# Retention rebuilt in groups of four, its weights loaded ahead, and the residual added by TensorE through a product with the identity

## The reference

```python
x = x + _L0_attn_ref(_layernorm(x), ...)
x = x + _L0_xattn_ref(_layernorm(x), ctx_2048, ctx_2048, Wh, wg_w, wo_w, gn_gamma, gn_beta)

def _L0_xattn_ref(x, k, v, Wh, wg_w, wo_w, gn_gamma, gn_beta):   # two heads of 128
    Q, K, V = xh @ Wh, kh @ Wh, vh @ Wh                # per head
    scores = einsum('bshe,bthe->bhst', Q, K) / sqrt(128)
    masked = scores * Dn[None]                         # decay mask
    A = maximum(abs(masked.sum(axis=0)), 1.0)          # summed over all batches
    O = einsum('hst,bthe->bshe', A, V).reshape(b, s, dim)
    Y = (O - mu) / sqrt(var + GN_EPS) * gn_gamma + gn_beta
    W = relu(x @ wg_w)
    return W * Y @ wo_w
```

## Time and profile before

| | us |
|---|---|
| median of 3 runs | 1221.38 |
| lowest and highest | 1221.18 and 1222.14 |
| the profiled execution | 1221.15 |
| its span in the trace | 1219.4 |
| from the end of attention's last product to the start of the spline stage | 124.2 |

### The profile page before, as it was taken

One profiled execution on the slowest core, in us unless ns is written; L12 is line 12 of the kernel. 1 busy time (PEld: TensorE's weight loads), 2 busy tenths in 40 slices (PEclk: granted clock), 3 DMA queues, 4 the chain that ended last, 5 costly groups with the idle time before them and its releaser, 6 DMA issues. The chain is left out here.

```text
span 1219.4 us, 19890 instructions
## 1 busy us (share of the span) xinstructions
PE 1049.1 (86%) x6765; PEld 853.8 (70%) x6765; DVE 811.5 (67%) x1513; ACT 721.8 (59%) x2021; POOL 340.2 (28%) x274
## 2 busy tenths in 40 slices
PE   3799999999999999999386778189999689698997
PEld 2678788888788888888285566176777489574555
DVE  3888777777587767667355867957777634355775
ACT  3577776777567776766133255157777434456883
POOL 1344332332233332333000630124444310101442
PEclk9999999999899999999799577669999989899999
DMA  5111100000000000000440000000000000004442
GB/s 173 53 52 54 35 1 1 2 1 2 1 1 1 1 1 1 1 1 1 118 107 1 0 1 1 0 1 2 1 2 1 2 1 1 14 1 122 108 109 69
DMA packets 31161, 31.78 MB, mean 26 GB/s; under 512 B 8288, under 2 KB 23392, under 8 KB 30816
## 3 DMA queue, kind: packets, MB, share of 16 engines
q1 hardware_dynamic: 31072, 30.60, 9.1%
HBM read 28.36 MB, written 2.23 MB: 25 GB/s over the span
## 5 line engine op out<-in xcount | busy, mean ns | idle before, releaser
L310 POOL TENSOR_TENSOR roped_q<-roped_q,sin_q 128x512 f32<-128x512 f32 x64 | 82.0, 1282 | 323.9 <-DVE sin_q L442 323.9
L35 PE MATMUL banks<-xT_lo,WH 128*128 128x512 f32 x256 | 107.8, 421 | 8.8 <-issue 6.2
L1411 ACT ACTIVATE win_P<-banks,win_neg_max 128x128 f32<-128x128 f32 x256 | 91.2, 381 | 33.1 <-DVE win_neg_max L1477 32.8
L310 POOL TENSOR_TENSOR roped_k<-roped_k,sin_k 128x512 f32<-128x512 f32 x64 | 95.7, 1496 | 53.0 <-DVE sin_k L442 53.0
L349 ACT ACTIVATE P<-banks,neg_max 128x128 f32<-128x128 f32 x256 | 90.5, 370 | 29.7 <-DVE neg_max L465 29.7
L36 PE MATMUL banks<-xT_hi,WL 128*128 128x512 f32 x256 | 102.5, 401 | 0.0
L37 PE MATMUL banks<-xT_hi,WH 128*128 128x512 f32 x256 | 102.4, 400 | 0.0
L376 ACT ACTIVATE oT_hi<-banks,bv_col 128x512 fp32r<-128x512 f32 x64 | 44.1, 689 | 87.6 <-PE banks L586 87.6
L1370 POOL TENSOR_TENSOR win_P<-win_P,win_inv 128x512 f32<-128x512 f32 x64 | 66.7, 1042 | 104.4 <-DVE win_inv L1482 104.1
L358 ACT ACTIVATE sin_k<-banks 64x512 f32<-64x512 f32 x128 | 76.0, 594 | 10.3 <-PE banks L37 8.7
L358 ACT ACTIVATE sin_q<-banks 64x512 f32<-64x512 f32 x128 | 76.0, 593 | 8.0 <-PE banks L37 5.8
(11 more groups left out here) (352 smaller groups left out, 3145.1 us busy)
## 6 DMA issues: line engine op xcount, KB each, us to landing
moe_gate_of<-moe_gate_rows SPq DMA_DIRECT2D x32, 256.0 KB, 4.0
X<-in_x SPq DMA_DIRECT2D x4, 512.0 KB, 6.7
stage<-in_wqT SPq DMA_DIRECT2D x4, 512.0 KB, 3.8
stage<-in_wkT SPq DMA_DIRECT2D x4, 512.0 KB, 3.8
stage<-in_wvT SPq DMA_DIRECT2D x4, 512.0 KB, 6.1
stage<-in_woT SPq DMA_DIRECT2D x4, 512.0 KB, 3.7
ctx<-in_ctxT SPq DMA_DIRECT2D x1, 2048.0 KB, 10.9
out<-X SPq DMA_DIRECT2D x8, 256.0 KB, 2.8
```

Source lines behind the costliest of these rows:

```text
L35: nc.tensor.matmul(out, lh, rl, start=first, stop=False)
L310: nc.gpsimd.tensor_tensor(roped[w][:, p, :], roped[w][:, p, :], sin_part[w][:], ALU.add).then_inc(roped_sum[w], 1)
L1411: ins = nc.scalar.activation(P[:, h % 2, s, i, :], SC[2 * (h % 2) + s][:, i * 128:(i + 1) * 128], ACT.Exp, bias=neg_max[:, h % 2, at:at + ...
```

## The change

Attention: the last group's `add_out` and `add_const` leave the attention block. At step 12 of the last group DVE computes mean and variance of the first 12 batches, and POOL their rstd behind its last step. The tile `stage`, the bias and one semaphore now outlive the block, and once the last attention weight is split SP loads the retention's five weight arrays into `stage`. The semaphores of attention are freed ahead of the retention.

Retention is one block, all of it written out without loops. The first pass goes by groups of four batches: the product with G is 512 columns wide and made of three split products; the transposed x is rounded and split right from PSUM; PE reads the context where it was loaded, and it comes in four transfers, one a group; V and the gate go by pairs of batches; the gate is stored multiplied by gamma (`gain`) and by beta (`shift`). The last group's attention sum, bias and statistics lie in DVE's stream inside the first group. The second pass goes by pairs: two DVE operations a batch give gate * (gamma * y + beta), POOL has no elementwise work left, and the residual is a first fp32 product `ident x X` into the bank in which the output projection is summed; ACT copies the sum to X.

```diff
@@ attention, SP, after the last weights
+                sp.wait_ge(weights_split, len(ITEMS))
+                held = stage[:].rearrange("p s k n -> p (s k n)")
+                for i, src in enumerate((chunks("L0_xattn_wg_w"), chunks("L0_xattn_wo_w"))):
+                    sp.dma_start(held[:, 512 * i:512 * (i + 1)].rearrange(...), src).then_inc(ret_loaded, 16)
+                for i, src in enumerate((a["WhT"], a["L0_xattn_Wh"]..., a["decayT"])):
+                    sp.dma_start(held[:, 1024 + 256 * i:1280 + 256 * i]..., src).then_inc(ret_loaded, 16)
@@ attention, DVE
+                    if r == 12 and isinstance(g, int) and g == NG - 1:
+                        dve.wait_ge(restated, NEXT)
+                        finish_stats(nc, dve, ln0, B + 22, stats[:, 0:NEXT, :], ...)
                 run(dve, step)
-                add_out(NG - 1)
-                add_const(NG - 1)
@@ retention, SP
-                    sp.dma_start(dst, src).then_inc(consts, 16)
-                sp.dma_start(ctx_all[:], ...).then_inc(ctx_loaded, 16)
+                for g in range(NG):
+                    sp.dma_start(ctx[:, :, g * GW:(g + 1) * GW], ...).then_inc(ctx_loaded[g], 16)
+                    if g == 0:
+                        for i, name in enumerate(("L0_xattn_gn_gamma", "L0_xattn_gn_beta")):
+                            sp.dma_start(gn[:, i, :], ...).then_inc(gn_loaded, 16)
                 for dst, src in ahead:
                     sp.dma_start(dst, src).then_inc(ahead_loaded, 16)
@@ retention, ACT
+                for g in range(NG):
+                    take_T(g)
+                    if g + 1 < NG:
+                        round_xT(g + 1)
+                        take_V(2 * g + 2)
+                        take_V(2 * g + 3)
+                for p in range(PAIRS):
+                    take_O(p)
+                for p in range(PAIRS + 1):
+                    if p < PAIRS:
+                        round_wyT(p)
+                    if p > 0:
+                        take_out(p - 1)        # PSUM sum -> X
@@ retention, DVE
+                normalise(0)
+                TT_(flat(G_lo[:]), VB[:, 0:256], flat(G_hi[:]).bitcast(F32), ALU.subtract)
+                add_heads()                    # last group's attention sum
+                split_xT(0)
+                split_w(0)
+                dve.wait_ge(gn_loaded, 32)
+                for g in range(NG):
+                    if g + 1 < NG:
+                        normalise(g + 1)
+                    take_gate(2 * g)           # two 512-wide operations
+                    if g + 1 < NG:
+                        split_xT(g + 1)
+                    if g == 0:
+                        add_out_bias()         # and the statistics of batches 12 to 15
+                    if g == NG - 1:
+                        dve.wait_ge(scored, NG)
+                        ...                    # A
+                    take_gate(2 * g + 1)
+                    if g == 0:
+                        dve.wait_ge(stat, GROUP)
+                        n = finish_stats(...)
+                        split_w(1)
+                group_stats(FIRST2); finish_stats(...)      # batches 0 to 3, POOL's power behind it
+                group_stats(REST2); finish_stats(...)       # batches 4 to 15
+                scale(0)
+                for p in range(PAIRS + 1):
+                    if p + 1 < PAIRS:
+                        scale(p + 1)
+                    if p < PAIRS:
+                        split_wyT(p)
+                    if p > 0:
+                        restat(p - 1)
@@ retention, PE
+                transpose_x(0)
+                pe.wait_ge(G_split, 1)
+                project_V(0)
+                project_V(1)
+                for g in range(NG):
+                    project_T(g)
+                    if g + 1 < NG:
+                        transpose_x(g + 1)
+                    project_gate(2 * g)
+                    if g + 1 < NG:
+                        project_V(2 * g + 2)
+                    score(g)
+                    project_gate(2 * g + 1)
+                    if g + 1 < NG:
+                        project_V(2 * g + 3)
+                for p in range(PAIRS):
+                    mix(p)
+                for p in range(PAIRS + 1):
+                    if p < PAIRS:
+                        transpose_wy(p)
+                    if p > 0:
+                        project_out(p - 1)
+                def project_out(p):
+                    wait(pe, added, p - 1)
+                    nc.tensor.matmul(WOB[p % 2], ident[:], flat(pair(X, p)), start=True, stop=False)
+                    pe.wait_ge(wyT_lo_ready, p + 1)
+                    ...                        # twelve split products, 256 columns each
```

More of the change, by code:

```diff
@@ new lines, in normalise, with add_heads @@
+                def normalise(g):
+                    wait(dve, x_transposed, g)
+                    if g * GROUP >= EARLY:
+                        dve.wait_ge(rstd_ready, 1)
+                    for i in range(GROUP):
+                        b = GROUP * g + i
+                        TS(xn[:, i, :], X[:, b, :], mean[:, b:b + 1], rstd[:, b:b + 1], ALU.subtract, ALU.mult).then_inc(xn_ready, 1)
+                def add_heads():
+                    for i in range(2):
+                        some = slice(EARLY + 2 * i, EARLY + 2 * i + 2)
+                        TT_(X[:, some, :], by_batch(OUT0[i]), X[:, some, :], ALU.add).then_inc(heads_added, 1)
@@ new lines, in add_out_bias @@
+                def add_out_bias():
+                    for i in range(2):
+                        some = slice(EARLY + 2 * i, EARLY + 2 * i + 2)
+                        dve.wait_ge(heads_added, i + 1)
+                        TT_(X[:, some, :], X[:, some, :], two(out_bias[:]), ALU.add).then_inc(heads_added, 1)
+                    dve.wait_ge(heads_added, 4)
+                    for b in range(EARLY, B):
+                        nc.vector.bn_stats(stats[:, b, :], X[:, b, :]).then_inc(stat, 1)
@@ new lines, in group_stats, with scale @@
+                def group_stats(some):
+                    for b in range(some.start, some.stop):
+                        dve.wait_ge(O_ready, b // 2 + 1)
+                        nc.vector.bn_stats(stats[:, b, :], O[:, b, :]).then_inc(stat2, 1)
+                def scale(p):
+                    dve.wait_ge(rstd2_ready, 1 if 2 * p + 1 < GROUP else 2)
+                    wait(dve, wy_transposed, p)
+                    for b in (2 * p, 2 * p + 1):
+                        STT(O[:, b, :], O[:, b, :], mean[:, b:b + 1], gain[:, b, :], ALU.subtract, ALU.mult).then_inc(scaled, 1)
+                    for b in (2 * p, 2 * p + 1):
+                        dve.wait_ge(scaled, b + 1)
+                        STT(xn[:, b % 2, :], O[:, b, :], rstd[:, b:b + 1], shift[:, b, :], ALU.mult, ALU.add).then_inc(wy_ready, 1)
@@ new lines, in project_gate @@
+                def project_gate(p):
+                    if p == 0:
+                        pe.wait_ge(w_split, 1)
+                        pe.wait_ge(heads_added, 2)
+                    wait(pe, gate_ready, 2 * (p - 1))
+                    for b in (2 * p, 2 * p + 1):
+                        g, toks = b // GROUP, slice(b % GROUP * S, (b % GROUP + 1) * S)
+                        for k in range(KD):
+                            ins = matmul3(nc, GATE[p % 2][:, b % 2 * D:(b % 2 + 1) * D], (xT_hi[:, g % 2, k, toks], xT_lo[:, g % 2, k, toks]),
+                                          (w_hi[:, 0, k, :], w_lo[:, 0, k, :]), first=(k == 0), last=(k == KD - 1))
+                    ins.then_inc(gate_made, 1)
@@ new lines, in mix, with transpose_wy @@
+                def mix(p):
+                    wait(pe, O_ready, p - 3)
+                    for h in range(H_):
+                        ins = nc.tensor.matmul(by_batch(MIX[p % 4])[:, :, h * 128:(h + 1) * 128], AT[:, h, :], V[:, 2 * p:2 * p + 2, h, :], start=True, stop=True)
+                    ins.then_inc(mixed, 1)
+                def transpose_wy(p):
+                    pe.wait_ge(wy_ready, 2 * p + 2)
+                    wait(pe, wyT_lo_ready, p - 1)
+                    for k in range(KD):
+                        for j in range(2):
+                            at = (2 * k + j) * 128
+                            ins = nc.tensor.transpose(WYB[p % 2][:, at:at + 128], xn[:, j, k * 128:(k + 1) * 128], ident[:])
+                    ins.then_inc(wy_transposed, 1)
```

426 lines of the change are left out of this document (191 added, 235 removed).

## The result

The changed kernel takes **1179.1 us** (median of four runs, 1177.49 to 1182.2) against 1221.55 before (1221.18 to 1222.14): a ratio of 0.9655, with a 95% interval of 0.9634 to 0.9676. The forecast was 1184.0, with 1177 to 1196 as its range, so it is 4.9 too high. The profiled execution took 1178.37, its span is 1176.3.

A forecast was written before the change was run, and what follows sets the result against it. Bounds by part: DVE, late loads, PE with batch hand-over, a chain, DVE. Terms 0.3 + 9.4 + 37.8 + 11.7 + 27.6 = 86.8 against 124.2, 37.4 saved: 1184.0 us, range 1177 to 1196.

The forecast's parts named there:

- a PEclk of 0.50 in the output pass: Sign of being wrong: TensorE at its lower clock in the output pass, which would point to rival A.
- rival C: Clock never falls at the seam; V, G and first output pair at the upper clock: 4 less, 1180; chance 0.14.
- The seam: End of attention: 4.24 us become a 0.3 barrier, as the last group's sum, bias and statistics move away.
- To the first product with G: Second part, 9.4 us against 15.2: context load 5.2, then V for pairs 0 and 1 at the lower clock 4.2.
- rival B: The loads are late: context takes as long as the old seven loads, V starts at 599.5, 1188; chance 0.13.
- First pass: Four groups on PE 32.1, lower clock at the first G product 1.5, waits 4.2: 37.8 us against 46.6.
- The 1.5 for a low clock at the start: First pass: the first product with G runs at the lower clock and adds 1.5 us.
- the place where the seam's work went: First group: DVE has 10.0 us in one queue before group 2's transposes, so PE waits 3.5.
- Turning point: Between the passes: mix 7.1, then ACT, statistics, mean and variance, scale and hand-overs: 11.7 us against 18.0.
- Output pass: Second pass: pairs 3.0 apart, seven distances 21.0, plus the end: 27.6 us against 40.2.
- rival A: Output pass stays at the lower clock: a pair takes 5.2 against 3.0, 18 more, 1202; chance 0.12.
- Behind the spline stage: From the spline stage's start on, the change touches nothing; any change of time there would be a sign of being wrong.

The follow-up runs named there:

- seam_back: Against the changed kernel, the last group's head sum, output bias and statistics go back to attention's end, ahead of the new block; 1185.15 us.
- after: The changed kernel itself, in its first profile; median 1179.1 us.
- after_again: The changed kernel run and profiled once more, nothing altered, as reference for its set; 1179.6 us.
- late_weights: Against the changed kernel, the five early weight loads go back to the start of the retention block, ahead of the context; 1184.87 us.
- keep_busy: Changed kernel plus seven unread identity products on TensorE: five behind the mix, two between the first two output transposes; 1180.05 us.
- residual_dve: Against the changed kernel, DVE adds the residual in place of the identity product and ScalarE's copy; 1181.98 us.
- best: Changed kernel with group 2 normalised before the bias, seven unread products filling PE's pauses, and DVE's residual for the last two pairs; 1175.24 us.

## Why the prediction was right, point by point

Right in its sum and range, by parts of which two missed in opposite directions; that retention came out at 86.6 for 86.8 is luck to that extent. By its own list, two signs of being wrong turned up beside the right ones: a PEclk of 0.50 in the output pass, for two pairs, and a change of time behind the spline stage's start. The measured 1179.1 is nearer to rival C's 1180 than to 1184.0, but only C's terms for V and G came true. Its third, the first output pair at the upper clock, didn't, and the sum held no low clock for that pair: by the sum's own terms C is worth 3.2, not 4.

1. **The seam: right.** SP's first load comes 0.42 behind attention's last product. seam_back shows what the move was worth: 3.6 to 4.0 us in the sum. Of the 4.2, 0.85 is paid back as PE's wait in the first group, and the clock at V and behind that wait makes up the rest.
2. **To the first product with G: 7.07 for 9.4.** The terms that failed are the context's landing (4.3 for 5.2) and the clock of V. The prediction's rival C had the clock of V and G so, but for a reason that doesn't hold: the clock did fall at the seam, only ahead of it. In after it is at 0.50 from 587.5 to 590.9, in attention's last products, and V ran at 1.00. In after_again, the same kernel, it fell later, behind a pause of only 1.33:

```profile
590.00:595.70 5.70, 3.01 (x22) 2.33 (x23) 4.90 (x11) 2.71 (x5) 0.00 (x0) 1.00 0.74 227
595.70:599.10 3.40, 3.40 (x13) 3.01 (x14) 1.11 (x4) 0.93 (x2) 0.00 (x0) 0.50 1.02 326
```

There the second half of V takes 2.01 for 1.16, and the first product with G is slow as the prediction had it. Where PE paused for 4.29, in seam_back, all of V ran at 0.50. late_weights confirms the loads as the term that carried this part, at 4.3 to 4.7; rival B would have needed a late context, and there was none.
3. **First pass: 37.37 for 37.8, by other terms.** The group is 8.71 apart, the next 13.20, then 9.31, and 6.15 for the last; forecast 8.7, 12.2, 9.4, 6.0. The wait is at its place and from its queue, 2.72 for 3.5. The 1.5 for a low clock at the start didn't come in this profile, and 1.6 to 1.8 for a low clock behind the wait came in its stead. In after_again it is the other way round, and the pass is 0.9 longer than late_weights' 35.8. By the prediction's own price of 0.21 for a split product the 1.5 would have been 1.1. The step that called the wait "the place where the seam's work went" is wrong for most of the wait: seam_back, without that work, still has 1.87 of the 2.72. The queue, added up to 10.0 us, took 9.0 (601.90 to 610.9), which is why the wait is shorter. The sum also left out that DVE can't take the second gate pair before PE has made it. In after it finds the pair ready (606.88); in seam_back, with less work ahead of it, it waits 1.69. In the later groups the sum has 0.7 for DVE, where its own 2.8 against 2.3 gives 0.5; PE waits 0.39.
4. **Turning point: 11.41 for 11.7.** The chain is as forecast and PE idles 4.23 in it; it is 11.3 to 11.4 in every variant.
5. **Output pass: 30.35 for 27.6.** The pairs at the upper clock are 3.0 apart on average, as forecast (the last five: 15.3 / 5 = 3.05). The failed term is the clock of the first two pairs: the second distance is 5.18, the very number that rival A gave a pair at the lower clock, for one pair and not for eight. keep_busy shows the pauses ahead of it as the cause. The rest is the end, 6.96 for 6.6. That the residual on TensorE would help the pass wasn't a term of its own in the sum. residual_dve shows that in this profile it didn't (30.0 without it), by what it costs at the lower clock and at the end; where the clock was low for equally long it gained 0.6.
The rule of the Trainium skill's page "TensorE: Matmul & The Clock Gate", Part 4, by which transposes don't count as busy the way products do, was weighed for A. The trace bears out no more than the forecast gave it: with four transposes in each pair, the clock was at 1.00 from 656 on.
6. **Behind the spline stage: forecast 0, measured 5.8 in this profile and 2.9 in after_again.** This is the step that failed, and it is most of what makes the forecast 4.9 us too high. The profiled span shrank by 43.0 where 37.4 was forecast: 37.6 in retention, 5.8 behind it, and attention was 0.35 longer. In after_again the miss is 4.1: 2.9 behind, 0.7 in retention, 0.55 in attention. That no instruction changes there was taken to mean that no time does. The prediction priced the clock inside retention with care and took its share behind retention to be unchanged.
The Trainium skill's page "TensorE: Matmul & The Clock Gate", Part 1, says that TensorE's clock gate watches PE's activity in windows that run free of the program. The traces agree as far as they can: equal code had the low clock at different points (0.84 and 0.71 over the same 25 us in the two profiles of the changed kernel).

What stays open: how much of the gain behind retention is the change's to keep. Before has 73.0 + 187.9, after 71.5 + 184.2 and 71.4 + 186.6, and best, a faster kernel in retention, has before's lengths again. Nor is it known what sets the moment. And the experiments take back only the seam, the loads and the residual. That the first pass, the turning point and the output pass are 9.3, 6.6 and 9.8 shorter through the wider products, the chain without POOL and the pairs is read from the traces before and after; no run undoes one of these alone.

## What to carry to other kernels

Find a queue's last item that the bottleneck waits for, and move it ahead of what nobody waits for; count the low clock that may follow such a pause with its price: here the same wait of 2.7 cost 2.9 us where the clock stayed up and 4.5 where it fell. An operation moved to an engine with room is worth what the moment's clock and the chain at the pass's end leave of it, so price it at both levels and at the last iteration. And when a stage gets shorter, look at the untouched stages behind it, in two profiles, before the gain is put down to the edit: here they gave or took 1 to 6 us.

## What the runs showed of the hardware

- At the seam, with pauses of PE of up to 1.74, the clock stayed at 1.00 over V in after and fell to 0.50 in the middle of V in after_again (595.7 to 599.1), where no pause was over 1.33. The wait of 2.7 in the first group was followed by the lower level in after (0.72 from 609 to 615) and by the upper one in after_again and late_weights. So for pauses up to this length it is not the pause alone that decides, even in one kernel. Pauses of 4.29 (seam_back) and 4.23 (turning point) were followed by 0.50 and 0.51.
- Products whose result nobody reads held the clock at 1.00 where the changed kernel pauses for 4.23 and 1.86, at a price of nothing on the path (the first transposes came 11.32 behind the first mixing product, 11.41 without).
- 1.0 us of extra DVE work ahead of the spline stage made the kernel 4.75 us slower by the medians, though one of its four runs was at 1177.5; 3.0 us less of output pass made it no faster.
- The identity product of 512 fp32 columns took 0.9 at the upper clock, the price of a mixing product, and 1.7 at the lower (start to start).
